# Layer 0 of a two-layer transformer kernel: the 4-bit weight codes unpacked in four groups of two pairs, and the second batch's preparation moved by a unit

## The chip, the cores and the metric

The kernel runs on one core of a Trainium2 chip, in one launch. The metric is the device time of a launch in microseconds. The engines are TensorE (PE), VectorE (DVE), ScalarE (ACT), GpSimd (POOL) and SyncE (SP), which issues the transfers.

## What is computed

Two layers, each an attention part and a feed-forward part on the same normalised input, over 8 batches of 256 tokens of width 256. The change touches layer 0 alone:

```python
xn = _layernorm(x)
# attention: 4 queries x 8 heads of width 8, K and V shared by the 4 queries
scores = einsum('bsqhd,bthd->bqhst', q, k) * scale
a_dot  = einsum('bqhst,bthd->bsqhd', softmax(scores), v)
a_mem  = elu(q) @ memory / (elu(q) @ memory_norm)
attn   = a_dot * (1 - w) + a_mem * w          # w = sigmoid(memory_weight)
# feed-forward: weights are 4-bit codes, two per byte, times a scale per 32
vals = LUT[stack([W & 15, W >> 4 & 15])] ; W = vals * scales
ffn  = (gelu(xn @ Wg.T) * (xn @ Wu.T)) @ Wd.T
x = x + attn + ffn
```

Layer 1 has another attention and a feed-forward with weights rounded to -1, 0 and 1 around a threshold taken from their mean absolute value. That mean is summed during layer 0.

## The kernel before

Layer 0 is a pipeline of **units**, one per batch and head: unit u works on batch u // 8 and head u % 8, and there are 64. Every engine runs its own program, a loop over u from `FIRST` = -3 to 66, and engines wait for one another by semaphores. In unit u TensorE does the exponentials' scores of unit u, the row scores of unit u + 2 (for the maximum), the gate and up products of chunk m = u - 1, the product with V of unit u - 1 and the down product of m - 2. ScalarE does the exponentials and the copies of high parts; VectorE the maxima (L593), the two GELU steps (L696, L704), the maxima's split into parts (L600, L602) and the normalisation (L612, L617); GpSimd multiplies hidden values (L345) and forms their low parts (L339). The split at L600 and L602, `split_max(u + 1)`, is the first thing that VectorE does in unit u, so in the text **unit u starts** at its L600, and unit u's length runs to the next L600. What TensorE does in a unit after its gate product waits for that split.

**Weights.** A pair a (0 to 7) is the 2 x 128 weight columns that chunk a uses. Its codes are 16-bit words, four codes each. `nibble_bits` (L620 on) moves the bits of the low and high codes into place as 8-bit floats; `decode(n)` (L638 on, n = 2a and 2a + 1) multiplies them by the loaded scales into an exact product of 768 columns; ScalarE copies its high part (L438) and GpSimd (L349, even n) and VectorE (L653, odd n) subtract to get the low part. Units -1 and 0 to 5 each decode one pair, and pair m is wanted by unit m + 1.

The bits are made in two halves of four pairs, each of five VectorE instructions over 1536 words: the first half at unit -3, two instructions of the second at the end of unit -1, the last two in unit 0. The codes lie in `probs`, a buffer of the exponentials, until they are spent; for that the exponential of unit 1 waits for `w_half` 5.

**A batch's preparation.** `schedule()` sets in which unit each step of a batch is done, on all engines: `stats` and `norm` (layer norm), `turn` (transposition on TensorE through the bank `misc`, high part by ScalarE, low part by VectorE at L543), `q`, `qlow`, `kv`, `mask0/1`, `recip0/1` (the division inside elu: L557, L559 on VectorE, L321, L324 on GpSimd), `mem` (two per batch, one for each 128 tokens: product with the memory into `misc`, L568 to L573 on VectorE) and `v` (V's transposition through `misc`). All steps in `FROM_MISC` use the same bank, so where a unit has two of them TensorE's second waits until the first has been read out (`evicted`):

```python
if before:
    evicted(*before)
...
elif kind == "mem":
    pe.wait_ge(S["mem_mul"], n + 1)
```

For batch 1 most steps stand a unit later than for the others (`late`), so that `mem` of batch 1 falls in units 8 and 9, and `v` in 9. From unit 9 to 17 VectorE also sums one piece of layer 1's weights (L684).

Of the kernel before, what the change touches and what calls it, by code (L numbers as in the profile page):

```python
# [15 lines left out]
P = 128  # L16
D = 256
# [57 lines left out]
SUM_AT, GAMMA_AT, SIGN_AT = 9, 21, 22  # L75
# [6 lines left out]
def schedule():  # L82

    at = {}

    def put(u, *step):
        at.setdefault(u, []).append(step)

    for kind in ("stats", "norm", "turn", "q", "qlow", "kv", "qload0", "mask0", "qload1", "mask1"):
        put(FIRST, kind, 0)  # L90
    put(-1, "recip0", 0)
    put(0, "recip1", 0)
    put(0, "v", 0)
    put(1, "mem", 0)
    put(2, "mem", 1)
    put(GAMMA_AT, "gamma", 0)
    for b in range(1, BATCH):
        late = int(b == 1)
        for n, kind in ((0, "stats"), (1, "norm"), (2 + late, "turn"), (3 + late, "q"), (4 + late, "qlow"), (4 + late, "qload0"), (4 + late, "kv"),
                        (5, "mask0"), (5 + late, "recip0"), (6 + late, "recip1"), (8, "qload1"), (8, "mask1")):  # L100
            put(HEADS * (b - 1) + n, kind, b)
        for t in range(2):
            put(HEADS * (b - 1) + 7 + late + t, "mem", 2 * b + t)
        put(HEADS * (b - 1) + 9, "v", b)
    for b in range(BATCH):
        put(HEADS * b + HEADS + 1, "att", b)
        put(HEADS * b + HEADS + LAG + BEHIND, "mlp", b)
    return at


def layer0(nc, dram, keep):
# [3 lines left out]
    with ExitStack() as ctx:  # L115
        def sb(name, shape, dt=F32):
# [43 lines left out]
        ones = sb("ones", [P, P])  # L160
# [6 lines left out]
        quarter = PAIRS_N * CW // 4  # L167
        codes, bits = ([spare[:, KC * 2 * D + quarter * n:KC * 2 * D + quarter * (n + 1)].bitcast(U16) for n in which] for which in ((0, 2), (1, 3)))
# [12 lines left out]
            codes0 codes1 stage0 stage1 w_half w2_hi_done w2_lo_even w2_lo_odd  # L181
# [20 lines left out]
        def _(sp):  # L202
# [10 lines left out]
            halves = dram["codes"].rearrange("p (h a) n -> p h (a n)", h=2)  # L213
            sp.dma_start(codes[0], halves[:, 0, :]).then_inc(S["codes0"], 16)
# [6 lines left out]
            sp.dma_start(codes[1], halves[:, 1, :]).then_inc(S["codes1"], 16)  # L221
# [80 lines left out]
        def _(pool):  # L302
# [6 lines left out]
            pool.memset(ones[:], 1.0).then_inc(S["zeroed"], 1)  # L309
# [55 lines left out]
            for u in range(FIRST, LAST):  # L365
                m = u - LAG
                if 0 <= m - 1 < M:
                    hidden_low(m - 1)
                if 0 <= m < M:
                    hidden(m)  # L370
                if 0 <= u + 2 < PAIRS_N and u >= 0:
                    weights_low(u + 2)
                for kind, n in at.get(u, []):
                    if kind == "mask1" and u == FIRST:
                        weights_low(0)
                    step(kind, n)
                    if kind == "recip0" and u == -1:
                        weights_low(1)
                i, odd = divmod(u - SIGN_AT - 1, 2)
                if 0 <= i < PIECES and not odd:  # L380
                    signs(i)

        @block.scalar
        def _(act):
# [3 lines left out]
            def step(kind, b):  # L388
# [10 lines left out]
                elif kind == "kv":  # L399
                    act.wait_ge(S["kv_done"], b + 1)  # L400
                    if b > 0:
                        for quad in range(2):
                            act.wait_ge(k_masked[quad], b)
                        act.wait_ge(S["v_turned"], b)
                    act.activation(kc[0:KROWS, :, :], misc[0:KROWS, :].rearrange("p (c n) -> p c n", c=2), ACT.Copy).then_inc(S["kv_copied"], 1)
                    act.activation(kc[KROWS:P, :, :].bitcast(F32), misc[KROWS:P, :].rearrange("p (c n) -> p c n", c=2), ACT.Copy).then_inc(S["kv_copied"], 1)
                elif kind == "v":
                    act.wait_ge(S["v_turned"], b + 1)
                    act.wait_ge(S["a_ready"], 4)
                    act.wait_ge(S["zeroed"], 5)  # L410
# [29 lines left out]
            def exponential(u, th):  # L440
                act.wait_ge(S["st_done"], 2 * u + th + 1)
                if u == 1 and th == 0:
                    act.wait_ge(S["w_half"], 5)
# [59 lines left out]
        def _(dve):  # L503
# [116 lines left out]
            def nibble_bits(half, n):  # L620

                at4 = slice(PAIRS_N // 2 * CW * half, PAIRS_N // 2 * CW * (half + 1))
                c, lo, hi, part = codes[half], low[:, at4], high[:, at4], bits[half]
                if n == 0:
                    dve.wait_ge(S[f"codes{half}"], 16)
                    dve.tensor_scalar(part, c, 2, 0x1C1C, ALU.logical_shift_left, ALU.bitwise_and).then_inc(S["dve_link"], 1)
                    dve.tensor_scalar(lo, c, 4, 0x8080, ALU.logical_shift_left, ALU.bitwise_and).then_inc(S["dve_link"], 1)
                    dve.wait_ge(S["dve_link"], linked(2))
                elif n == 1:
                    dve.tensor_tensor(lo, lo, part, ALU.bitwise_or).then_inc(S["dve_link"], 1)  # L630
                    dve.wait_ge(S["dve_link"], linked())
                elif n == 2:
                    dve.tensor_scalar(part, c, 2, 0x1C1C, ALU.logical_shift_right, ALU.bitwise_and).then_inc(S["dve_link"], 1)
                    dve.wait_ge(S["dve_link"], linked())
                else:
                    dve.scalar_tensor_tensor(out=hi, in0=c, scalar=0x8080, in1=part, op0=ALU.bitwise_and, op1=ALU.bitwise_or).then_inc(S["dve_link"], 1)
                    dve.wait_ge(S["dve_link"], linked())
# [24 lines left out]
            for u in range(FIRST, LAST):  # L662
                m = u - LAG
                if u == FIRST:
                    for kind, n in at[u]:
# [4 lines left out]
                        if kind == "turn":  # L670
                            for k in range(4):
                                nibble_bits(0, k)
# [52 lines left out]
        def _(pe):  # L725
# [33 lines left out]
            def step(kind, b):  # L759
# [1081 lines left out]
```

## Time and profile before

| | |
|---|---|
| time, median of 3 runs (lowest, highest) | 938.91 us (937.0, 942.07) |
| the profiled execution's own time | 938.2 us |
| its span | 936.4 us |
| PE busy | 763.0 us, 81% of the span |
| DVE busy | 699.5 us, 75% |
| ACT busy | 452.4 us, 48% |
| POOL busy | 419.0 us, 45% |
| instructions | 15623 |

The span is that of the engines in the profile; the run takes 1.8 us more around it. Layer 0 takes the first two thirds of the span. A row of the view in order of time gives start and duration, engine, line, operation, what is written and read, and in brackets how long the engine had been idle before, and what ended the wait.

### The profile page before, as it was taken

How to read it: one execution, taken by the hardware profiler on the slowest of the kernel's cores; microseconds unless marked ns; L12 is line 12 of the kernel's file. 1: busy time of each engine (PE TensorE's matmuls, PEld its weight loads, DVE VectorE, ACT ScalarE, POOL GpSimd, SP SyncE). 2: the span in 40 equal slices, each digit the busy share in tenths (PEclk: the TensorE clock that was granted, in tenths of full speed). 3: DMA queues.
4: the chain of work that ended last, by engine and by line, in shares of the span. 5: the costliest groups of instructions: out<-in, count | busy, mean ns of one | idle time of the engine just before them, and what ended most of it. 6: DMA issues, size and time to landing. Idle time of an engine off the chain costs nothing. (4 is left out here: it accounts for less than half of the span.)

```text
span 936.4 us, 15623 instructions
## 1 busy us (share of the span) xinstructions
PE 763.0 (81%) x5602; PEld 653.7 (70%) x5602; DVE 699.5 (75%) x1146; ACT 452.4 (48%) x717; POOL 419.0 (45%) x335
## 2 busy tenths in 40 slices
PE   3278989999999999999999999918683883893842
PEld 3166878888888888888888888806572672682642
DVE  6988866876776766776776766346689889879866
ACT  4256546556657556557556565535342342332301
POOL 2244533443466756662542543342616616606622
PEclk9999989999999999999999999958796896796775
DMA  4111210110110110110000000030000000000000
GB/s 150 34 35 36 86 42 25 53 42 2 30 36 19 47 42 19 47 30 3 20 18 12 11 19 3 1 147 1 1 1 0 8 15 0 0 22 0 0 22 23
DMA packets 21383, 25.82 MB, mean 28 GB/s; under 512 B 4418, under 2 KB 17090, under 8 KB 21060
## 3 DMA queue, kind: packets, MB, share of 16 engines
q1 hardware_dynamic: 21316, 24.93, 9.0%
q8 instruction: 41, 0.67, 0.3%
q14 instruction: 26, 0.21, 0.1%
HBM read 14.83 MB, written 3.28 MB: 19 GB/s over the span
## 5 line engine op out<-in xcount | busy, mean ns | idle before, releaser
L593 DVE TENSOR_REDUCE neg_max<-s_pair 128x4 f32<-128x1024 f32 x127 | 155.0, 1220 | 81.4 <-PE s_pair L805 81.1
L446 ACT ACTIVATE probs<-t_pair 128x1024 f32<-128x1024 f32 x128 | 131.3, 1026 | 139.8 <-PE t_pair L830 139.6
L345 POOL TENSOR_TENSOR hid<-g,hid 128x512 f32<-128x512 f32 x64 | 82.3, 1286 | 185.5 <-DVE g L704 143.9
L339 POOL TENSOR_TENSOR hid_lo<-hid,hid_hi 128x512 fp32r<-128x512 f32 x64 | 85.9, 1342 | 96.1 <-ACT hid_hi L456 96.0
L805 PE MATMUL s_pair<-K,Q 96*128 96x256 f32 x508 | 85.5, 292 | 14.0 <-DVE neg_max L593 9.4
L805 PEld LDWEIGHTS s_pair<-K,Q 96*128 96x128 f32 x508 | 76.6, 196 | 22.8 <-issue 7.3
L830 PE MATMUL t_pair<-Q,K 104*128 104x512 f32 x256 | 86.5, 420 | 0.3 <-DMA Q<-max_parts 0.3
L872 PE MATMUL down<-w_hi,hid_hi 128*128 128x256 f32 x256 | 83.9, 328 | 0.7 <-POOL hid_lo L339 0.7
L872 PE MATMUL down<-w_lo,hid_hi 128*128 128x256 f32 x256 | 72.1, 282 | 0.0
L872 PE MATMUL down<-w_hi,hid_lo 128*128 128x256 f32 x256 | 72.1, 282 | 0.0
L1151 POOL TENSOR_TENSOR rows<-rows,par 128x512 f32<-128x512 f32 x24 | 36.2, 1509 | 79.5 <-DVE rows L1499 52.4
L845 PE MATMUL misc<-probs,V 128*32 128x256 f32 x1024 | 69.1, 388 | 0.8 <-DVE xn_lo L543 0.5
L872 PEld LDWEIGHTS down<-w_hi,hid_hi 128*128 128x128 f32 x256 | 48.2, 188 | 26.4 <-issue 24.7
L1641 PE MATMUL lbank<-l_xn_hi,tern 128*128 128x512 f32 x96 | 38.0, 484 | 25.1 <-DVE l_hid L1469 25.1
L733 PE MATMUL gate<-xn_hi,w_hi 128*128 128x256 f32 x256 | 56.9, 304 | 0.0
L696 DVE SCALAR_TENSOR_TENSOR g<-g,gate 128x512 f32<-128x512 f32 x64 | 42.7, 668 | 18.6 <-ACT g L459 18.5
L467 ACT ACTIVATE g<-g 128x512 f32<-128x512 f32 x64 | 40.2, 628 | 26.6 <-DVE g L696 26.6
L733 PE MATMUL up<-xn_hi,w_hi 128*128 128x256 f32 x256 | 52.8, 289 | 0.0
L733 PE MATMUL up<-xn_lo,w_hi 128*128 128x256 f32 x256 | 52.3, 286 | 0.0
L733 PE MATMUL up<-xn_hi,w_lo 128*128 128x256 f32 x256 | 52.3, 287 | 0.0
L733 PE MATMUL gate<-xn_hi,w_lo 128*128 128x256 f32 x256 | 51.4, 282 | 0.0
L733 PE MATMUL gate<-xn_lo,w_hi 128*128 128x256 f32 x256 | 51.3, 282 | 0.0
(244 smaller groups left out, 2058.2 us busy)
## 6 DMA issues: line engine op xcount, KB each, us to landing
stage<-in_ternary SPq DMA_DIRECT2D x18, 256.0 KB, 2.9
Q<-q_hi SPq DMA_DIRECT2D x64, 64.0 KB, 2.0
stage<-in_scales SPq DMA_DIRECT2D x8, 384.0 KB, 3.4
X<-in_x SPq DMA_DIRECT2D x8, 256.0 KB, 3.7
Q<-q_lo SPq DMA_DIRECT2D x32, 64.0 KB, 2.0
Q<-max_parts SPq DMA_DIRECT2D x128, 4.0 KB
out<-res SPq DMA_DIRECT2D x8, 256.0 KB, 2.2
shared<-in_l1w SPq DMA_DIRECT2D x1, 1536.0 KB, 6.2
```

The lines of the kernel that those rows point to most:

```text
L339: pool.tensor_tensor(hid_lo[:, m % 2, :, :].rearrange("p a n -> p (a n)"), hid[:, m % 2, :], hid_hi[:, m % 2, :, :].rearrange("p a n -> p ...
L345: pool.tensor_tensor(hid[:, m % 2, :], g[:, m % 2, :], hid[:, m % 2, :], ALU.mult).then_inc(S["hid_done"], 1)
L446: act.activation(probs[:, u % 2, th, :], t_pair[:], ACT.Exp, scale=SCALE).then_inc(S["probs_done"], 1)
L467: act.activation(g[:, m % 2, :], g[:, m % 2, :], ACT.Tanh, scale=GELU_B).then_inc(S["t_done"], 1)
L593: dve.tensor_reduce(neg_max[:, u % 2, 4 * jp:4 * jp + 4], score_banks(u, jp)[:].rearrange("p (s n) -> p s n", n=SEQ), AX_X, ALU.max, negat ...
L696: dve.scalar_tensor_tensor(out=g[:, m % 2, :], in0=g[:, m % 2, :], scalar=1.0, in1=gate[:], op0=ALU.add, op1=ALU.mult).then_inc(S["u_done" ...
L733: mm = pe.matmul(out, lhs[a][k], rhs[b][k], start=(n == 0), stop=(n == 3 * KC - 1))
L805: mm = pe.matmul(score_banks(u, jp)[:, 512 * j + SEQ * s:512 * j + SEQ * s + SEQ], Q[0:KROWS, quad, 2 * jp + j, P * s:P * s + P], K[0:KROW ...
L830: mm = pe.matmul(t_pair[:, 512 * jp:512 * jp + 512].rearrange("p (j n) -> p j n", j=2), K[rows, quad, hq, P * th:P * th + P], Q[rows, quad ...
L845: mm = pe.matmul(misc[32 * j:32 * j + 32, 0:SEQ], V[:, th, h, :], probs[:, u % 2, th, SEQ * j:SEQ * j + SEQ], start=(th == 0), stop=(th == ...
L872: mm = pe.matmul(down[:, D * t:D * t + D], h[:, m % 2, n, P * t:P * t + P], w[:, a, n, 2 * D:3 * D], start=(a == 0 and t == 0 and n == 0 a ...
L1641: mm = pe.matmul(banks[bank][:], w[:, k, P * c:P * c + P], x[:, k, :], start=(n == 0), stop=(n == 3))
```

## The change

- The codes come by one transfer of 768 KB into `high` (in `X`, where the high bits are made in place) in place of two of 384 KB into `probs`. The transfer is fifth in SyncE's queue as the first half was.
- `nibble_bits(a)` handles two pairs: the same five instructions over 768 words, in `part`, a scratch of its own. It is called for pairs 0 and 1 in unit -3, for 2 and 3 at the end of unit -1, for 4 and 5 at the end of unit 1, for 6 and 7 at the end of unit 3, in the last two ahead of the unit's L653.
- In unit -1 `weights_low(1)` on VectorE follows the decodes at once. The memory's weights are scaled in unit 0.
- `schedule()`: batch 0's `recip0` in unit 0, `recip1` and `v` in 1, `mem` in 2 and 3 (before -1, 0, 0, 1 and 2). Batch 1's `stats` in unit 1 and `norm` in 2 (before 0 and 1); its `recip0`, `recip1` in 5 and 6 (before 6 and 7) and its `mem` in 7 and 8 (before 8 and 9). `turn`, `q`, `kv` and the masks stay.
- The sums of layer 1's weights begin in unit 10. `ones` lies in `part`, set when the weights are done. The exponential of unit 1 has no wait for `w_half`.

```diff
-SUM_AT, GAMMA_AT, SIGN_AT = 9, 21, 22
+SUM_AT, GAMMA_AT, SIGN_AT = 10, 21, 22
...
-    put(-1, "recip0", 0)
-    put(0, "recip1", 0)
-    put(0, "v", 0)
-    put(1, "mem", 0)
-    put(2, "mem", 1)
+    put(0, "recip0", 0)
+    put(1, "recip1", 0)
+    put(1, "v", 0)
+    put(2, "mem", 0)
+    put(3, "mem", 1)
...
-        for n, kind in ((0, "stats"), (1, "norm"), (2 + late, "turn"), (3 + late, "q"), (4 + late, "qlow"), (4 + late, "qload0"), (4 + late, "kv"),
-                        (5, "mask0"), (5 + late, "recip0"), (6 + late, "recip1"), (8, "qload1"), (8, "mask1")):
+        for n, kind in ((late, "stats"), (1 + late, "norm"), (2 + late, "turn"), (3 + late, "q"), (4 + late, "qlow"), (4 + late, "qload0"), (4 + late, "kv"),
+                        (5, "mask0"), (5, "recip0"), (6, "recip1"), (8, "qload1"), (8, "mask1")):
...
-            put(HEADS * (b - 1) + 7 + late + t, "mem", 2 * b + t)
+            put(HEADS * (b - 1) + 7 + t, "mem", 2 * b + t)
...
-            halves = dram["codes"].rearrange("p (h a) n -> p h (a n)", h=2)
-            sp.dma_start(codes[0], halves[:, 0, :]).then_inc(S["codes0"], 16)
+            sp.dma_start(high, dram["codes"].rearrange("p a n -> p (a n)")).then_inc(S["codes_loaded"], 16)
...
-            sp.dma_start(codes[1], halves[:, 1, :]).then_inc(S["codes1"], 16)
...
-                if u == 1 and th == 0:
-                    act.wait_ge(S["w_half"], 5)
...
+            def nibble_bits(a):
+
+                lo, hi = (x[:, CW * a:CW * a + 2 * CW] for x in (low, high))
+                dve.wait_ge(S["codes_loaded"], 16)
+                dve.tensor_scalar(part[:], hi, 2, 0x1C1C, ALU.logical_shift_left, ALU.bitwise_and).then_inc(S["dve_link"], 1)
+                dve.tensor_scalar(lo, hi, 4, 0x8080, ALU.logical_shift_left, ALU.bitwise_and).then_inc(S["dve_link"], 1)
+                dve.wait_ge(S["dve_link"], linked(2))
+                dve.tensor_tensor(lo, lo, part[:], ALU.bitwise_or).then_inc(S["dve_link"], 1)
+                dve.wait_ge(S["dve_link"], linked())
+                dve.tensor_scalar(part[:], hi, 2, 0x1C1C, ALU.logical_shift_right, ALU.bitwise_and).then_inc(S["dve_link"], 1)
+                dve.wait_ge(S["dve_link"], linked())
+                dve.scalar_tensor_tensor(out=hi, in0=hi, scalar=0x8080, in1=part[:], op0=ALU.bitwise_and, op1=ALU.bitwise_or).then_inc(S["dve_link"], 1)
+                dve.wait_ge(S["dve_link"], linked())
...
-                if u == 0:
-                    nibble_bits(1, 2)
-                    nibble_bits(1, 3)
...
                 if u == -1:
                     decode(2)
                     decode(3)
+                    weights_low(1)
+                    nibble_bits(2)
+                if u == 0:
                     memory_weights()
-                    for kind, n in at[u]:
-                        step(kind, n)
-                    weights_low(1)
-                    nibble_bits(1, 0)
-                    nibble_bits(1, 1)
+                if u in (1, 3):
+                    nibble_bits(u + 3)
                 if 0 <= u < PAIRS_N - 2:
                     weights_low(u + 2)
```

How the order moves, at three places. First VectorE from unit -1's decodes and the memory's weights to unit 0's, before (rows on probs and X of 1536 are the bits, xn<-q_neg is `recip`, stats and mv are `stats`):

```order
L557 TENSOR_SCALAR xn<-q_neg 128x256
L559 RECIPROCAL xn<-xn 128x256
L653 TENSOR_TENSOR w_lo<-hid,w_hi 128x768
L626 TENSOR_SCALAR probs<-probs 128x1536
L627 TENSOR_SCALAR X<-probs 128x1536
L630 TENSOR_TENSOR X<-X,probs 128x1536
L600 CAST max_parts<-misc 8x128
L602 TENSOR_TENSOR max_parts<-misc,max_parts 8x128
L557 TENSOR_SCALAR xn<-q_neg 128x256
L559 RECIPROCAL xn<-xn 128x256
L529 BN_STATS stats<-X 128x6 x2
L532 BN_AGGR mv<-stats 128x2 x2
```

After these come the last of the bits' instructions and the decodes.

VectorE now, from the same decodes of unit -1 (w_stage and hid are unit 0's `decode`):

```order
L645 TENSOR_TENSOR w_lo<-hid,w_hi 128x768
L621 TENSOR_SCALAR part<-X 128x768
L622 TENSOR_SCALAR X<-X 128x768
L624 TENSOR_TENSOR X<-X,part 128x768
L626 TENSOR_SCALAR part<-X 128x768
L628 SCALAR_TENSOR_TENSOR X<-X,part 128x768
L597 CAST max_parts<-misc 8x128
L599 TENSOR_TENSOR max_parts<-misc,max_parts 8x128
L554 TENSOR_SCALAR xn<-q_neg 128x256
L556 RECIPROCAL xn<-xn 128x256
L640 SCALAR_TENSOR_TENSOR w_stage<-X,stage 128x768
L640 SCALAR_TENSOR_TENSOR hid<-X,stage 128x768
```

The low part comes first, the bits are one group of 768, and one `recip` is left ahead of unit 0's decodes, where before `recip1`, `stats` and two of the bits' instructions stood.

Second, GpSimd from unit 0 to 2, before (q_neg and sigma are `recip`, rstd is `stats`, hid the hidden product, w_lo the low part of the weights):

```order
L321 TENSOR_TENSOR q_neg<-q_neg,xn 128x256
L324 TENSOR_TENSOR sigma<-sigma,q_neg 128x256
L315 TENSOR_SCALAR rstd<-mv 128x2
L317 TENSOR_TENSOR rstd<-rstd,half 128x2
L345 TENSOR_TENSOR hid<-g,hid 128x512
L349 TENSOR_TENSOR w_lo<-w_stage,w_hi 128x768
L339 TENSOR_TENSOR hid_lo<-hid,hid_hi 128x512
```

Both steps of `recip1` and the two of `stats` stand ahead of unit 1's hidden product. GpSimd now:

```order
L317 TENSOR_TENSOR q_neg<-q_neg,xn 128x256
L320 TENSOR_TENSOR sigma<-sigma,q_neg 128x256
L341 TENSOR_TENSOR hid<-g,hid 128x512
L345 TENSOR_TENSOR w_lo<-w_stage,w_hi 128x768
L317 TENSOR_TENSOR q_neg<-q_neg,xn 128x256
L320 TENSOR_TENSOR sigma<-sigma,q_neg 128x256
L311 TENSOR_SCALAR rstd<-mv 128x2
L313 TENSOR_TENSOR rstd<-rstd,half 128x2
L335 TENSOR_TENSOR hid_lo<-hid,hid_hi 128x512
```

`recip1` and `stats` have moved behind the hidden product and the low part of unit 1.

Third, TensorE in unit 3 now (mem is `mem`, ident with xn is `turn`):

```order
L721 MATMUL gate<-xn_lo,w_hi 128x256 x2
L775 MATMUL misc<-mem,sigma 128x130 x2
L752 MATMUL misc<-ident,xn 128x128 x4
L818 MATMUL t_pair<-Q,K 128x512 x2
L793 MATMUL s_pair<-K,Q 128x256 x4
```

Before, the row on mem stands in unit 2, and the row on xn follows the gate product. TensorE in unit 9 before (ident with kc is `v`):

```order
L733 MATMUL gate<-xn_lo,w_hi 128x256 x2
L787 MATMUL misc<-mem,sigma 128x130 x2
L781 MATMUL misc<-ident,kc 128x32 x4
L830 MATMUL t_pair<-Q,K 128x512 x2
L805 MATMUL s_pair<-K,Q 128x256 x4
```

Two steps use `misc` one after the other. Unit 9 now:

```order
L721 MATMUL gate<-xn_lo,w_hi 128x256 x2
L769 MATMUL misc<-ident,kc 128x32 x4
L818 MATMUL t_pair<-Q,K 128x512 x2
L793 MATMUL s_pair<-K,Q 128x256 x4
L721 MATMUL up<-xn_hi,w_hi 128x256 x2
```

A second step through `misc` stood in unit 9 and stands in unit 3 now.

## Rows read from the trace of the kernel before

**Rows 1.** Busy time by stretch; columns as the first line names them

```profile
core 0: us, PE busy (x) PEld busy (x) DVE busy (x) ACT busy (x) POOL busy (x), PEclk, DMA share, GB/s
60.00:70.00 10.00, 7.15 (x60) 5.74 (x59) 9.62 (x15) 6.20 (x10) 4.90 (x4) 1.00 0.14 40
...
134.00:136.00 2.00, 1.42 (x6) 1.26 (x7) 0.91 (x3) 0.37 (x1) 0.00 (x0) 0.50 0.00 0
```

**Rows 2.** VectorE's instructions in time, first half of the code bits (start, duration, us)

```profile
9.22 0.55 DVE L626 TENSOR_SCALAR probs<-probs 128x1536 uint16<-128x1536 uint16 x1
...
11.86 1.76 DVE L636 SCALAR_TENSOR_TENSOR X<-probs 128x1536 uint16<-128x1536 uint16 x1
13.71 0.69 DVE L547 TENSOR_TENSOR q_lo<-sigma,q_hi 128x512 fp32r<-128x512 f32 x1
```

**Rows 3.** VectorE's instructions in time, units -1 and 0

```profile
30.87 0.95 DVE L648 SCALAR_TENSOR_TENSOR hid<-X,stage 128x768 f32<-128x768 fp8e4 x1
...
32.38 0.29 DVE L557 TENSOR_SCALAR xn<-q_neg 128x256 f32<-128x256 f32 x1
...
34.37 0.90 DVE L653 TENSOR_TENSOR w_lo<-hid,w_hi 128x768 fp32r<-128x768 f32 x1
35.18 1.07 DVE L626 TENSOR_SCALAR probs<-probs 128x1536 uint16<-128x1536 uint16 x1
...
39.76 0.28 DVE L600 CAST max_parts<-misc 8x128 fp32r<-8x128 f32 x1
...
40.29 0.27 DVE L557 TENSOR_SCALAR xn<-q_neg 128x256 f32<-128x256 f32 x1
...
43.15 0.53 DVE L633 TENSOR_SCALAR probs<-probs 128x1536 uint16<-128x1536 uint16 x1
...
45.50 0.96 DVE L648 SCALAR_TENSOR_TENSOR w_stage<-X,stage 128x768 f32<-128x768 fp8e4 x1
...
52.19 0.28 DVE L600 CAST max_parts<-misc 8x128 fp32r<-8x128 f32 x1 [0.26 <-PE misc L817]
```

**Rows 4.** ScalarE's instructions in time, unit -1

```profile
31.85 0.84 ACT L438 ACTIVATE w_hi<-hid 128x768 fp32r<-128x768 f32 x1
```

**Rows 5.** VectorE's instructions in time, unit 1

```profile
52.71 0.72 DVE L539 TENSOR_SCALAR xn<-X,mv,rstd 128x256 f32<-128x256 f32 x2
...
56.08 0.42 DVE L570 TENSOR_TENSOR a_mem<-misc,a_rec 128x256 f32<-128x256 f32 x1
...
60.44 2.23 DVE L653 TENSOR_TENSOR w_lo<-X,w_hi 128x768 fp32r<-128x768 f32 x1
62.60 0.27 DVE L600 CAST max_parts<-misc 8x128 fp32r<-8x128 f32 x1
```

**Rows 6.** GpSimd's instructions in time, units 0 and 1

```profile
49.19 0.73 POOL L321 TENSOR_TENSOR q_neg<-q_neg,xn 128x256 f32<-128x256 f32 x1
...
51.09 1.40 POOL L317 TENSOR_TENSOR rstd<-rstd,half 128x2 f32<-128x2 f32 x1
...
60.03 1.83 POOL L349 TENSOR_TENSOR w_lo<-w_stage,w_hi 128x768 fp32r<-128x768 f32 x1
61.82 1.97 POOL L339 TENSOR_TENSOR hid_lo<-hid,hid_hi 128x512 fp32r<-128x512 f32 x1
```

**Rows 7.** TensorE's instructions in time, units 3 and 9

```profile
73.36 0.66 PE L764 MATMUL misc<-ident,xn 128*128 128x128 f32 x4 [1.61 <-DVE max_parts L602]
...
134.58 0.63 PE L781 MATMUL misc<-ident,kc 32*128 32x32 f32 x4 [3.58 <-DVE a_mem L570]
```

**Rows 8.** VectorE's instructions in time, units 4, 8 and 9

```profile
89.55 1.23 DVE L593 TENSOR_REDUCE neg_max<-s_pair 128x4 f32<-128x1024 f32 x1 [1.90 <-PE s_pair L805]
...
121.24 0.28 DVE L600 CAST max_parts<-misc 8x128 fp32r<-8x128 f32 x1 [0.63 <-PE misc L817]
...
129.64 0.28 DVE L600 CAST max_parts<-misc 8x128 fp32r<-8x128 f32 x1 [0.63 <-PE misc L817]
...
144.63 0.28 DVE L600 CAST max_parts<-misc 8x128 fp32r<-8x128 f32 x1 [0.62 <-PE misc L817]
```

More of the change, by code:

```diff
@@ L159, in layer0 @@
         below, sign = (w_stage[:].bitcast(BF16)[:, PIECE * n:PIECE * n + PIECE] for n in range(2))
-        ones = sb("ones", [P, P])
         hid_flat = hid[:].rearrange("p a n -> p (a n)")[:, 0:WORDS]
@@ L166, in layer0 @@
         w_raw = spare[:, 0:KC * 2 * D].rearrange("p (k n) -> p k n", k=KC)
-        quarter = PAIRS_N * CW // 4
-        codes, bits = ([spare[:, KC * 2 * D + quarter * n:KC * 2 * D + quarter * (n + 1)].bitcast(U16) for n in which] for which in ((0, 2), (1, 3)))
+        part = sb("part", [P, 2 * CW], U16)
+        ones = part[:, 0:2 * P].bitcast(F32)
         s_pair = ctx.enter_context(nc.psum_tensor("s_pair", [P, 1024], F32))
@@ L180, in layer0 @@
             gate_done up_done sq_done u_done t_done v1_done up_copied hid_done hid_hi_done hid_lo_done down_done
-            codes0 codes1 stage0 stage1 w_half w2_hi_done w2_lo_even w2_lo_odd
+            codes_loaded stage0 stage1 w_half w2_hi_done w2_lo_even w2_lo_odd
             summed gamma signed stored dve_link pool_link""".split()
@@ L308, in _ @@
             pool.memset(V[:, :, :, DH:DH + 1], 1.0).then_inc(S["zeroed"], 1)
-            pool.memset(ones[:], 1.0).then_inc(S["zeroed"], 1)
             def step(kind, b):
@@ L376, in _ @@
                     step(kind, n)
-                    if kind == "recip0" and u == -1:
-                        weights_low(1)
+                if u == -1:
+                    weights_low(1)
+                if u == SUM_AT:
+                    pool.wait_ge(S["w_half"], 2 * PAIRS_N)
+                    pool.memset(ones, 1.0).then_inc(S["zeroed"], 1)
                 i, odd = divmod(u - SIGN_AT - 1, 2)
@@ L409, in step @@
                     act.wait_ge(S["a_ready"], 4)
-                    act.wait_ge(S["zeroed"], 5)
+                    act.wait_ge(S["zeroed"], 4)
                     if b > 0:
@@ L618, in normalised @@
                                   ALU.mult).then_inc(S["o_normed"], 1)
[L620 to L637, printed above, removed]
+            def nibble_bits(a):
[10 more added lines that the diff above has]
+                dve.wait_ge(S["dve_link"], linked())
             def decode(n):
@@ L670, in _ @@
                         if kind == "turn":
-                            for k in range(4):
-                                nibble_bits(0, k)
+                            nibble_bits(0)
                     decode(0)
@@ L678, in _ @@
                 for kind, n in at.get(u, []):
-                    if kind not in FROM_MISC and u >= 0:
+                    if kind not in FROM_MISC:
                         step(kind, n)
@@ L713, in _ @@
                     decode(3)
+                    weights_low(1)
+                    nibble_bits(2)
+                if u == 0:
                     memory_weights()
-                    for kind, n in at[u]:
-                        step(kind, n)
-                    weights_low(1)
-                    nibble_bits(1, 0)
-                    nibble_bits(1, 1)
+                if u in (1, 3):
+                    nibble_bits(u + 3)
                 if 0 <= u < PAIRS_N - 2:
@@ L792, in step @@
                     pe.wait_ge(S["zeroed"], 5)
-                    pe.matmul(misc[:, 0:3], ones[:], gsum[:], start=True, stop=True).then_inc(S["gamma"], 1)
+                    pe.matmul(misc[:, 0:3], ones, gsum[:], start=True, stop=True).then_inc(S["gamma"], 1)
             def scores(u, jp):
```

## The prediction

> **What bounds the kernel now.** I read the view by stretch first: from 60 to 70 us VectorE is busy for 9.62 of 10 us and TensorE for 7.15 [rows 1]. So while the weights are being prepared (units -1 to 5) VectorE sets the pace, and an instruction added to it moves all that follows. The view in order of time then shows its rows without a bracket, that is with no wait ahead, for most of that stretch [rows 3, 5]; the exceptions are short (0.26 us at unit 1's start) or are TensorE's (1.90 us in unit 4) [rows 3, 8]. Behind these units the two engines hand one another their results, and a unit takes 8.40 us (unit 8, from 121.24 to 129.64). Unit 9 takes 14.99 us [rows 8]. TensorE's row tells why: it stood 3.58 us for `mem`'s multiplication on VectorE before it could use the bank again, and from 134 to 136 us its granted clock is 0.50, the 1.2 GHz level [rows 7, 1]. Layer 0 is one chain of units, so a unit's gain or loss arrives whole at the end. I add up, unit by unit, how far the start of each (its L600) moves against the profiled execution's own 938.2 us. The median of the runs is 0.7 us above that.
>
> **The price of a group.** One half now takes from 9.22 to 13.62 us, 4.40 us in five instructions [rows 2]. Its last takes 1.76 us for 1536 words, and a decode of 768 takes 0.95 [rows 2, 3], so the work halves and some 0.15 us per instruction stays: (4.40 - 0.75) / 2 + 0.75 = 2.6 us a group. The Trainium skill ("VectorE: DVE Perf Modes", section on the TRN2 errata) gives a fixed term of 58 cycles, 60 ns, per instruction; by it a group would be 2.35 us as an estimate and the sum 0.8 us less for the three groups that end up on the path. The trace shows more than that.
>
> **Unit -3.** The first group begins at 9.22 and ends at 11.8. The next instruction, q_lo, waits for ScalarE in any case and began at 13.71 [rows 2]. Gain: nothing. What covers it, 1.9 us, also covers a codes transfer that is twice as long, should it land late. The 768 KB load is ahead of the scales in SyncE's queue, but those are first used by the decodes, well behind q_lo.
>
> **Unit -1.** Decode ends at 31.82 [rows 3]. ScalarE's high part is done at 31.85 + 0.84 = 32.69 [rows 4], so `weights_low(1)` now waits 0.9 us where the memory's weights and `recip0` stood. It also meets GpSimd's low part, which takes 1.83 us and would run to 33.7. VectorE's subtraction took 0.90 us alone [rows 3] and 2.23 us where it met that one, ending 0.81 us after GpSimd's end at 61.86 [rows 5, 6]. So here it ends at 34.5, the second group at 37.1. Unit 0 starts 2.7 us **earlier** (before: 39.76 [rows 3]).
>
> **Unit 0.** Split 0.53 (39.76 to 40.29), one `recip` 1.99 (32.38 to 34.37), the memory's weights 0.56 (31.82 to 32.38), and what stood from 45.50 to 52.19 without its 0.26 wait, 6.43 [rows 3]: 9.5 us. Unit 1 starts at 46.6, 5.6 us **earlier**. That is where half the bits, `recip1` and `stats` have gone.
>
> **Unit 1.** Before, from 52.19 to 60.44, 8.25 us [rows 3, 5]. Out go `norm` (0.65) and `mem` (two of 0.42 and a small one, 1.0) [rows 5]; in come `recip1` and `stats`, 2.86 (40.29 to 43.15 [rows 3]): 9.5 us, to 56.1, a lead of 4.3 us. Now the third group and the low part follow, 3.5 us alone. But GpSimd has its queue at that moment: the hidden product and low part, which ended 1.42 us after this point before (61.86 against 60.44), so at 57.5 now; then `recip1` and `stats`, 3.3 us in the trace with some of it in collision (49.19 to 52.49), some 2.5 us free; then hid_lo, some 1.3 us free, 1.97 where it collides [rows 6]. All are operations that collide with VectorE's on SBUF. Taken strictly in turns from 57.5, 3.8 of GpSimd and 3.5 of VectorE end at 64.8; with no more collision than before it is 61.0. I take 63.7, near the first, because the order now puts five GpSimd instructions beside six of VectorE. Unit 2 starts 1.1 us **later** (-1.6 to +2.2; before 62.60 [rows 5]).
>
> **Unit 2.** `norm` comes in, GpSimd's collision at its start goes, TensorE starts at its low clock: +0.3 (0 to 1.2).
>
> **Unit 3, `mem` and `turn` together.** TensorE's second step must wait for VectorE's decodes, first GELU step and `mem`, about 4.1 us after the unit's start. It is unit 9's arrangement, which cost 14.99 - 8.40 = 6.6 us with the wait ending 4.9 us after the start [rows 7, 8]; 0.8 us less wait, and a little for the part of `turn` that was there, gives +5.5. Of this 3.0 is the wait itself, the rest the clock. A gap of 1.61 us ahead of the same `turn` did not halve the clock before: its four transposes took 0.66 us [rows 7]. Now the gap is nearly 3 us, with one short product ahead of it and 1.6 us of idle ahead of that. The fourth group adds 2.6 and some 0.2 of collision (up to 3.7). Unit 3: +8.3.
>
> **Unit 4.** It is TensorE's (1.90 us of VectorE waiting [rows 8]). The fourth group lets TensorE stand some 5 us before the unit starts, so its products begin at 1.2 GHz: +2.3 (0 to 3), a third of the 6.5 us from the split to the row at 89.55.
>
> **Units 5 to 9.** `recip0` of batch 1 comes into unit 5, 1.99 us, partly in a wait: +1.3 (0.6 to 2.0). Unit 6 exchanges one `recip` for the other: 0. Unit 7 gets a `mem`, 1.0, and loses a `recip` that was in a wait: +0.7 (0 to 1.0). Unit 8: the same length. Unit 9 keeps only `v` on the bank, as do later batches' units; I take it back to unit 8's length: **-6.6** (-6.0 to -6.9). Moving the sums by a unit, the scratch and the dropped exponential wait: 0, each beside other work.
>
> **Sum.** 1.1 + 0.3 + 5.5 + 2.8 + 2.3 + 1.3 + 0.7 - 6.6 = +7.4 us: 938.2 + 7.4 = **945.6 us**.
>
> **Rivals.**
> 1. *TensorE keeps its clock in units 3 and 4.* Then unit 3 loses 3.0 instead of 5.5 and unit 4 nothing: +2.6, **940.8 us**. For it: the 1.61 us gaps that left the clock up. Against it: the 3.58 us gap in unit 9 that did not. The decisive point is whether a broken gap of 3 us counts as one. The Trainium skill ("TensorE: Matmul & The Clock Gate", section on HAM oscillation) has the clock fall only when the idle stretch crosses a whole window of the gate, whose phase is free; by it this rival could be right in one run and wrong in another, at the same 940.8 us. Chance 0.22.
> 2. *Faster: the last two groups fall into time in which VectorE would have waited.* The lead of 4.3 us at the end of unit 1 is then kept: -4.3 + 0.3 + 3.0 + 1.3 + 0.7 - 6.6 = -5.6, **932.6 us**. It decides on whether VectorE has 2.6 us of waiting in units 1 and 3. Against it: 9.62 of 10 us busy, and no bracket at 60.44 or 62.60 [rows 1, 5]. For it: unit 3 will wait for TensorE anyhow, but ahead of the group and not where it stands. Chance 0.12.
> 3. *Slower still:* full turn-taking in units 1 and 3 and a low clock carried into unit 5: +2.2 + 1.2 + 5.8 + 3.7 + 3 + 2 + 1 - 6.0 = +12.9, **951 us**. Chance 0.06.
> 4. *It does not do what it says:* a code transfer later than its cover of 1.9 us, which would delay unit -2 by the rest. It is in the chance of the third.
>
> **How the numbers follow.** The forecast has 0.60. About 0.5% (4.7 us, 934.2 to 943.6) is what a measurement here can tell from no change. Faster: rival 2, 0.12. Same: rival 1 and the low edge of the forecast, 0.22 + 0.04 = 0.26. Slower: 0.56 + 0.06 = 0.62. The range takes in the forecast's bounds and most of rival 1: 939 to 950 us; left out are rival 2 and the far end, under 0.2.
>
> **What would show it.** Unit 0 should start near 37.1, unit 1 near 46.6, unit 2 near 63.7 with bits' instructions of twice their length beside GpSimd rows, unit 4 some 10 us later than before; TensorE's `turn` in unit 3 should wait for a_mem near 3 us with a granted clock of 0.50 behind it; unit 9 should be near 8.4 us. I am wrong if unit 1's end stays early, if unit 3 has no second wait, or if unit 9 stays at 15 us.

## The result and the profile after

| | before | changed |
|---|---|---|
| time, median (lowest, highest), 20 runs each | 937.08 us (933.3, 942.07) | 944.32 us (940.85, 949.73) |
| ratio of the mean times, 95% interval | | 1.0086 [1.0066, 1.0106] |
| the profiled execution's own time | 938.2 us | 949.73 us |

The changed kernel is slower by 0.9% (by 7.2 us, 0.8%, between the medians), and the whole interval lies above the 0.5% that a measurement here can tell. Its page begins:

```profile
span 947.8 us, 15633 instructions
...
PE 764.8 (81%) x5602; PEld 654.2 (69%) x5602; DVE 701.3 (74%) x1156; ACT 452.4 (48%) x717; POOL 416.6 (44%) x335
```

VectorE does 1.8 us more than before, TensorE 1.8 us: the work hardly grew. The profiled execution happens to be the longest of the 20, and its span is 11.4 us longer than before's. 3.1 us of that lie behind layer 0, where no instruction differs: from the start of unit 62 to the end of the span the trace has 352.0 us, before's 348.9, and those of the experiments below 345.6 to 351.0. So I compare layer 0, by the starts of its units (L597 here, L600 before). Unit 62 starts 8.3 us later than before, and all of that is there when unit 10 starts. Lengths in us, from one start to the next, and the sum of forecasts for the same units:

| unit | -1 | 0 | 1 | 2 | 3 | 4 | 5 | 6 | 7 | 8 | 9 |
|---|---|---|---|---|---|---|---|---|---|---|---|
| before | 13.93 | 12.43 | 10.41 | 10.12 | 9.71 | 11.24 | 11.16 | 8.72 | 7.69 | 8.40 | 14.99 |
| changed | 11.24 | 9.36 | 16.11 | 11.45 | 17.88 | 12.76 | 13.09 | 10.24 | 8.37 | 8.40 | 8.28 |
| difference | -2.7 | -3.1 | +5.7 | +1.3 | +8.2 | +1.5 | +1.9 | +1.5 | +0.7 | 0 | -6.7 |
| forecast | -2.7 | -2.9 | +6.7 | +0.3 | +8.3 | +2.3 | +1.3 | 0 | +0.7 | 0 | -6.6 |

The differences add up to +8.4 us, the forecasts to +7.4.

**Units -3 to 0.** VectorE's instructions in time (start, duration, what is written and read, in brackets the wait ahead):

```profile
9.21 0.35 DVE L621 TENSOR_SCALAR part<-X 128x768 uint16<-128x768 uint16 x1
...
10.85 0.96 DVE L628 SCALAR_TENSOR_TENSOR X<-X,part 128x768 uint16<-128x768 uint16 x1
13.70 0.69 DVE L544 TENSOR_TENSOR q_lo<-sigma,q_hi 128x512 fp32r<-128x512 f32 x1 [1.90 <-ACT q_hi L421]
...
32.72 1.80 DVE L645 TENSOR_TENSOR w_lo<-hid,w_hi 128x768 fp32r<-128x768 f32 x1 [0.91 <-ACT w_hi L437]
34.43 0.35 DVE L621 TENSOR_SCALAR part<-X 128x768 uint16<-128x768 uint16 x1
...
37.06 0.28 DVE L597 CAST max_parts<-misc 8x128 fp32r<-8x128 f32 x1
...
46.42 0.27 DVE L597 CAST max_parts<-misc 8x128 fp32r<-8x128 f32 x1
```

A group takes 2.63 us (34.43 to 37.06). In unit -3 q_lo starts where it did [rows 2] and the gain turns into 1.90 us of waiting, so the longer transfer was in time as well.

**Unit 1.** VectorE, then GpSimd, in time:

```profile
55.87 1.62 DVE L621 TENSOR_SCALAR part<-X 128x768 uint16<-128x768 uint16 x1
57.41 0.88 DVE L622 TENSOR_SCALAR X<-X 128x768 uint16<-128x768 uint16 x1
58.33 0.96 DVE L624 TENSOR_TENSOR X<-X,part 128x768 uint16<-128x768 uint16 x1
59.32 0.36 DVE L626 TENSOR_SCALAR part<-X 128x768 uint16<-128x768 uint16 x1
59.72 0.96 DVE L628 SCALAR_TENSOR_TENSOR X<-X,part 128x768 uint16<-128x768 uint16 x1
60.71 1.90 DVE L645 TENSOR_TENSOR w_lo<-X,w_hi 128x768 fp32r<-128x768 f32 x1
62.53 0.27 DVE L597 CAST max_parts<-misc 8x128 fp32r<-8x128 f32 x1
```

```profile
55.44 1.84 POOL L345 TENSOR_TENSOR w_lo<-w_stage,w_hi 128x768 fp32r<-128x768 f32 x1
57.22 0.85 POOL L317 TENSOR_TENSOR q_neg<-q_neg,xn 128x256 f32<-128x256 f32 x1
58.15 0.72 POOL L320 TENSOR_TENSOR sigma<-sigma,q_neg 128x256 f32<-128x256 f32 x1
58.96 0.38 POOL L311 TENSOR_SCALAR rstd<-mv 128x2 f32<-128x2 f32 x1
59.42 0.82 POOL L313 TENSOR_TENSOR rstd<-rstd,half 128x2 f32<-128x2 f32 x1
60.21 1.59 POOL L335 TENSOR_TENSOR hid_lo<-hid,hid_hi 128x512 fp32r<-128x512 f32 x1
```

The first instruction of the bits lasts 1.62 us in place of 0.35 and ends 0.2 us after GpSimd's low part (57.28). The Trainium skill ("SBUF — State Buffer", section "Who interferes with whom") says that where a VectorE instruction in one of its two-port modes meets one of GpSimd's, the one issued first keeps the shared ports to its end and the other waits; no row names the mode, but the length of this one agrees. The first three meet GpSimd and lose 2.2 us together, the low part 1.0; the fourth and fifth lose nothing, though `rstd`'s two small instructions stand beside them, and `hid_lo` begins beside the fifth. For the group and the low part VectorE took 6.7 us, where 3.5 would have done.

**Units 2 and 3.** TensorE in time, its stretches, and VectorE in time:

```profile
63.17 1.24 PE L775 MATMUL misc<-mem,sigma 128*128 128x130 f32 x4 [6.14 <-DVE max_parts L599]
...
74.62 0.71 PE L775 MATMUL misc<-mem,sigma 128*128 128x130 f32 x4 [1.10 <-DVE max_parts L599]
78.07 1.12 PE L752 MATMUL misc<-ident,xn 128*128 128x128 f32 x4 [2.74 <-DVE a_mem L567]
```

```profile
76.00:78.00 2.00, 0.00 (x0) 0.00 (x0) 1.97 (x4) 0.00 (x0) 0.00 (x0) 0.61 0.00 0
78.00:80.00 2.00, 1.93 (x7) 1.74 (x8) 0.59 (x3) 0.60 (x1) 0.00 (x0) 0.50 0.00 0
...
82.00:84.00 2.00, 2.00 (x19) 1.58 (x22) 0.76 (x2) 0.54 (x1) 0.00 (x0) 0.69 0.68 169
```

```profile
70.84 1.22 DVE L590 TENSOR_REDUCE neg_max<-s_pair 128x4 f32<-128x1024 f32 x1 [2.00 <-PE s_pair L793]
...
85.84 1.23 DVE L590 TENSOR_REDUCE neg_max<-s_pair 128x4 f32<-128x1024 f32 x1 [3.09 <-PE s_pair L793]
...
100.50 1.23 DVE L590 TENSOR_REDUCE neg_max<-s_pair 128x4 f32<-128x1024 f32 x1 [2.29 <-PE s_pair L793]
```

The new second wait is there: 2.74 us for `mem`'s multiplication on VectorE, after which the granted clock is 0.50 (1.2 GHz) and `turn`'s four transposes take 1.12 us where they took 0.66 [rows 7]. Unit 2 has a slow clock too (0.50 from 60 to 68 us): TensorE had stood 6.14 us while VectorE finished unit 1, its `mem` takes 1.24 us against 0.71 in unit 3, and VectorE waits 2.00 us for the scores at the unit's end.

**Unit 9.** VectorE's rows of two successive starts:

```profile
144.72 0.28 DVE L597 CAST max_parts<-misc 8x128 fp32r<-8x128 f32 x1 [0.63 <-PE misc L805]
...
153.00 0.28 DVE L597 CAST max_parts<-misc 8x128 fp32r<-8x128 f32 x1 [0.63 <-PE misc L805]
```

8.28 us, where it was 14.99 [rows 8]: the stall is gone from here.

### The profile page after: what moved, and what is told of

Same layout as the page of the kernel before. It is cut to its first block and busy times, and to the rows that moved or that the text cites. A ratio compares the mean times of both kernels' runs of the same rounds, so it can differ in the third digit from the quotient of the medians.

```text
span 947.8 us, 15633 instructions
## 1 busy us (share of the span) xinstructions
PE 764.8 (81%) x5602; PEld 654.2 (69%) x5602; DVE 701.3 (74%) x1156; ACT 452.4 (48%) x717; POOL 416.6 (44%) x335
## 3 DMA queue, kind: packets, MB, share of 16 engines
HBM read 14.83 MB, written 3.28 MB: 19 GB/s over the span
```

## The experiments

My theory: the time is set by *where* the steps stand. A step pair in one unit through `misc` costs some 6.6 us with its clock (gone in unit 9, new in unit 3), and bits that stand beside GpSimd's queue lose time in turns; the halved work of a group gains what it can only in the units before 1. The rival: TensorE's clock is the main price (rival 1 of the prediction with its sign turned), so that keeping it would take most of the loss away. A second rival: it is the mere number of instructions, fixed parts included, wherever they stand. In the tables "layer 0" is how far the start of unit 10 moves against before, counted from the start of unit -1; it is +8.4 us for the changed kernel. 1.5 us of this, in unit 6, come and go with the moment (last section); where a comparison needs it, they are taken out, which leaves +6.9.

### Batch 1's steps by themselves

Onto the kernel before (`b1early`), and taken back out of the changed one (`a_b1late`):

```diff
-                        (5, "mask0"), (5 + late, "recip0"), (6 + late, "recip1"), (8, "qload1"), (8, "mask1")):
+                        (5, "mask0"), (5, "recip0"), (6, "recip1"), (8, "qload1"), (8, "mask1")):
...
-            put(HEADS * (b - 1) + 7 + late + t, "mem", 2 * b + t)
+            put(HEADS * (b - 1) + 7 + t, "mem", 2 * b + t)
```

> The kernel before with one part of the change alone: batch 1's two reciprocals in units 5 and 6 and its mem in 7 and 8. Theory (a second step through the bank in unit 9 held TensorE for VectorE's mem): unit 9 falls from 15.0 to 8.9 us (it keeps its piece of the sum), unit 5 grows by 1.9, unit 7 by 0.7; in all 3.5 us faster, ratio 0.996. Rival (unit 9 is long for the sum and the layer norm there): unit 9 stays over 13 us and the kernel is 1 to 3 us slower, ratio 1.002.

> The changed kernel with that same part undone: batch 1's reciprocals in 6 and 7, mem in 8 and 9. Theory: unit 9 goes back to some 14.4 us (no sum in it), units 5 and 7 lose 1.9 and 0.7: some 3.5 us slower than the changed kernel, layer 0 some 12 us longer than before, ratio to before 1.012. Rival (the gain in unit 9 came from the sum that moved to unit 10): unit 9 stays under 9 us and the kernel is 2.6 us faster than the changed one, ratio 1.006.

| | median | ratio to before | units 5, 6, 7, 9 | layer 0 |
|---|---|---|---|---|
| b1early | 935.17 us | 0.9958 [0.9936, 0.9981] | 13.08, 10.18, 8.38, 8.54 | -2.4 us |
| a_b1late | 948.44 us | 1.0094 [1.0067, 1.0121] | 11.15, 8.72, 7.68, 14.83 | +10.4 us |

This part alone makes the kernel faster, and without it layer 0 is longer still in the trace (+10.4 us). The ratios of `a_b1late` and of the changed kernel, 1.0094 and 1.0086, don't tell these two apart; 1.012 had been expected. Unit 9 gives 6.5 us in both; unit 5 takes 1.9, unit 7 0.7 and unit 6 1.5 of it back. In `a_b1late` TensorE has the second wait of unit 9 again:

```profile
144.54 0.63 PE L769 MATMUL misc<-ident,kc 32*128 32x32 f32 x4 [2.98 <-DVE a_mem L567]
```

### Batch 0's preparation back where it was

```diff
-    put(0, "recip0", 0)
-    put(1, "recip1", 0)
-    put(1, "v", 0)
-    put(2, "mem", 0)
-    put(3, "mem", 1)
+    put(-1, "recip0", 0)
+    put(0, "recip1", 0)
+    put(0, "v", 0)
+    put(1, "mem", 0)
+    put(2, "mem", 1)
...
-                    if kind not in FROM_MISC:
+                    if kind not in FROM_MISC and u >= 0:
                         step(kind, n)
...
                     weights_low(1)
+                    memory_weights()
+                    for kind, n in at[u]:
+                        step(kind, n)
                     nibble_bits(2)
-                if u == 0:
-                    memory_weights()
```

> The changed kernel with batch 0's steps where they were before (reciprocals in units -1 and 0, v in 0, mem in 1 and 2), the bits still in four groups. Theory (mem and turn of unit 3 on one bank, and GpSimd's steps beside the bits in unit 1): unit 3 falls from 17.9 to about 12.5, unit 1 from 16.1 by 2.9 for the reciprocal and by some 1 for the collision while 1.0 comes back with mem; units -1 and 0 grow by 2.6 and 0. Layer 0 is 1 to 2.5 us longer than before, ratio 1.002. Rival (the groups of bits alone are what costs): unit 3 stays over 16 us and layer 0 is 7 to 8 us longer than before, ratio 1.008.

942.02 us, ratio 1.004 [1.0011, 1.0069], layer 0 +5.3 us. Unit 3 takes 13.30 us in place of 17.88: 4.6 us for the second step through `misc`, in the same unit and with the same group of bits. Units 1 and 2 are shorter too, by 1.8 and 1.0, and unit -1 is longer by 4.2. In all, the later preparation of batch 0 costs 3.1 us. The expectation had 1 to 2.5 us for layer 0 and missed it: unit 3 stays 0.8 us above the expected 12.5, and unit -1 grows by 4.2 in place of 2.6.

### The bits alone

`a_b0early` with batch 1's schedule of before, `stats` and `norm` included, so that the groups of two pairs are nearly all that is left of the change:

```diff
-        for n, kind in ((late, "stats"), (1 + late, "norm"), (2 + late, "turn"), (3 + late, "q"), (4 + late, "qlow"), (4 + late, "qload0"), (4 + late, "kv"),
-                        (5, "mask0"), (5, "recip0"), (6, "recip1"), (8, "qload1"), (8, "mask1")):
+        for n, kind in ((0, "stats"), (1, "norm"), (2 + late, "turn"), (3 + late, "q"), (4 + late, "qlow"), (4 + late, "qload0"), (4 + late, "kv"),
+                        (5, "mask0"), (5 + late, "recip0"), (6 + late, "recip1"), (8, "qload1"), (8, "mask1")):
...
-            put(HEADS * (b - 1) + 7 + t, "mem", 2 * b + t)
+            put(HEADS * (b - 1) + 7 + late + t, "mem", 2 * b + t)
```

> The bits in four groups over the schedule of the kernel before, with every batch step where it was. Theory (the four groups cost more than the two halves because the third and fourth stand on VectorE at the ends of units 1 and 3, and TensorE's clock falls in the gaps they make): units -1 and 0 together 1.8 us shorter, unit 1 3.9 longer, unit 3 3.6, unit 4 1.9, unit 9 15 us as before; layer 0 some 8 us longer, ratio 1.008. Rival (the groups cost little by themselves, the loss is all in the schedule): ratio within 1.002.

945.95 us, ratio 1.0075 [1.005, 1.01], layer 0 +9.7 us. Against before: unit -1 +1.5, unit 0 -2.4, unit 1 +3.7, unit 2 +1.1, unit 3 +3.6, unit 4 +2.3. The two halves cost VectorE 2 x 4.4 us at free lengths and four groups 4 x 2.63 = 10.5, 1.7 us more. But the first half stood in unit -3, where it cost nothing (q_lo starts at 13.7 us with the half and with the group), and of the four groups only one does. On the path there were 4.4 us and are 3 x 2.63 = 7.9, so 3.5 of the 9.7 us are instructions. The other 6 are waits and collisions, and hang on where the groups stand; the next runs test that.

### The same bits in another place

`a_bits0` moves the third and fourth group to the end of unit 0. `a_bits0pool1` has GpSimd, besides, do unit 1's steps ahead of its hidden product, and `a_pool1` does that alone.

```diff
-                if u in (1, 3):
-                    nibble_bits(u + 3)
+                if u == 0:
+                    nibble_bits(4)
+                    nibble_bits(6)
```

```diff
+                if u == 1:
+                    for kind, n in at[u]:
+                        step(kind, n)
                 if 0 <= m - 1 < M:
                     hidden_low(m - 1)
                 if 0 <= m < M:
                     hidden(m)
...
-                    step(kind, n)
+                    if u != 1:
+                        step(kind, n)
```

> The changed kernel with the third and fourth groups at the end of unit 0, where GpSimd is idle and no chunk has begun. Theory (place, not work): unit 0 grows by two groups, 5.0 us; unit 1 falls by 2.6 and some 1.0 of collision, unit 3 by 3.6 with what collided, unit 4 by 1 to 2 for TensorE's clock: 3 to 4 us faster than the changed kernel, ratio 1.005. Rival (only the sum of instructions counts): no change against the changed kernel, ratio 1.0086.

> The changed kernel with GpSimd doing recip1 and stats of unit 1 ahead of that unit's hidden product, when it is idle. No work changes. Theory (VectorE's bits in unit 1 wait for GpSimd's instructions one by one): the bits' first three instructions lose their long durations but one, unit 1 falls from 16.1 to about 14.8, ratio to before 1.007. Rival (the bits are slow for another reason, such as the new scratch): unit 1 stays 16.1.

> Both edits at once: the third and fourth groups at the end of unit 0, and GpSimd's recip1 and stats of unit 1 ahead of its hidden product. Theory (in the kernel with the groups in unit 0, unit 2 took 13.2 us because norm waited 1.97 us for GpSimd's stats behind its hidden product and low part, and mem's product for recip1): unit 2 falls from 13.2 to about 10.8, layer 0 by 2 to 2.5 us against that kernel, ratio to before 1.002. Rival (unit 2 was long for TensorE's clock alone): unit 2 stays over 12.5 us and the ratio is 1.0045.

| | median | ratio to before | units 0, 1, 2, 3, 4 | layer 0 |
|---|---|---|---|---|
| a_bits0 | 941.29 us | 1.0046 [1.0019, 1.0073] | 14.64, 11.59, 13.21, 14.15, 11.24 | +4.6 us |
| a_pool1 | 945.33 us | 1.0061 [1.0035, 1.0086] | 9.35, 15.64, 11.16, 17.76, 12.75 | +7.5 us |
| a_bits0pool1 | 937.41 us | 0.9996 [0.9977, 1.0015] | 14.65, 11.93, 10.65, 13.86, 11.23 | +2.1 us |

No instruction of the changed kernel is taken away in any of the three, and the last is 0.9% faster than it, level with the kernel before, where 1.002 had been expected: the second rival (number of instructions) falls. In `a_bits0` all ten instructions of the two groups have their free lengths. Unit 1 is 4.5 us shorter, unit 3 3.7, unit 4 1.5; unit 0 is 5.3 longer, unit 2 is 1.8 longer, and units 5 and 6 together are 0.5 longer than with unit 6's clock kept. So the place is worth 2 us, and 4.8 with the next edit. Unit 2 grows since its `norm` now waits for what GpSimd has last in its queue:

```profile
65.98 1.68 DVE L536 TENSOR_SCALAR xn<-X,mv,rstd 128x256 f32<-128x256 f32 x2 [1.97 <-POOL rstd L313]
```

With GpSimd's steps moved ahead, in `a_bits0pool1`, that row has no wait:

```profile
64.12 1.16 DVE L540 TENSOR_SCALAR xn<-X,mv,rstd 128x256 f32<-128x256 f32 x2
```

`a_pool1` missed its expectation for unit 1: 15.64 us, where 14.8 had been expected. VectorE's first two of the bits there:

```profile
56.58 1.61 DVE L625 TENSOR_SCALAR part<-X 128x768 uint16<-128x768 uint16 x1
58.11 1.42 DVE L626 TENSOR_SCALAR X<-X 128x768 uint16<-128x768 uint16 x1
```

The number of GpSimd instructions beside them fell from six to two, but GpSimd's two long ones (the low parts of the weights, 1.83 us, and of the hidden values, 1.38 us) each hold one of VectorE's short ones, 2.3 us together. After them everything is at free length. With six beside them VectorE lost 3.2 us, with two 2.3. So most of the cost goes with the long instructions that one meets, and little with how many there are.

### TensorE kept busy in unit 3

22 products with a discarded result stand between `mem` and `turn`, in the 2.7 us of waiting:

```diff
                     if before:
+                        if u == 3:
+                            pe.wait_ge(S["up_copied"], u - LAG)
+                            for _ in range(22):
+                                pe.matmul(up[:, 0:SEQ], w_hi[:, 0, 0, 0:P], xn_hi[:, 0, 0, :], start=True, stop=True)
                         evicted(*before)
```

> The changed kernel with 22 products added on TensorE in unit 3, into the bank up, in the time in which it waits for VectorE's mem. Their result is overwritten unread. Theory (of the 8 us by which unit 3 grew some 2.5 are TensorE's clock): the granted clock stays 1.00 from 74 to 84 us and unit 3 falls from 17.9 to about 15.4, ratio to before 1.006. Rival (the clock lies beside VectorE's work and costs nothing): unit 3 keeps 17.9 us or grows by the products that run past the wait, ratio 1.009 or more.

946.21 us, ratio 1.0078 [1.0049, 1.0107], which can't be told from the changed kernel's 1.0086. TensorE in time, and its stretch, with this edit:

```profile
73.55 2.88 PE L876 MATMUL up<-xn_hi,w_hi 128*128 128x256 f32 x22
76.54 0.66 PE L752 MATMUL misc<-ident,xn 128*128 128x128 f32 x4
```

```profile
78.00:80.00 2.00, 2.00 (x26) 1.70 (x28) 2.00 (x3) 1.64 (x3) 0.00 (x0) 1.00 0.02 4
```

The clock stays up, and unit 3 is 15.57 us in place of 17.88. So of the 4.6 us of that unit's second step 2.3 are the clock; the rest I put down to the wait. But unit 4 takes 13.99 us in place of 12.76: half of the gain is lost again there. TensorE stands 3.75 us ahead of it in both kernels, and with the edit the granted clock is down at once (0.51 from 88 to 90 us; 0.87 from 92 to 94 us in the changed kernel); why it fell sooner no run shows. The profiled execution is also the fastest of its six (939.9 us), so its units can't be read as those of the median. The rival falls: with the clock kept in unit 3 (and, by chance, in unit 6) layer 0 is still 5.3 us longer than before.

### A version that beats both

`best1` takes what has been shown to be good: the kernel before with `b1early`'s edit, and the bits of unit -1 ahead of `recip0` and the low part, where GpSimd has nothing to do yet:

```diff
                     memory_weights()
+                    nibble_bits(1, 0)
+                    nibble_bits(1, 1)
                     for kind, n in at[u]:
                         step(kind, n)
                     weights_low(1)
-                    nibble_bits(1, 0)
-                    nibble_bits(1, 1)
```

> The kernel before with batch 1's reciprocals and mem a unit earlier, and in unit -1 the two instructions' worth of bits ahead of recip0 and the low part, so that GpSimd is idle beside them. Theory: the bits' three instructions fall from 4.6 to 2.1 us, the low part gains some of it back by meeting GpSimd's; unit -1 some 1.5 to 2 us shorter on top of the 3.9 of the schedule: ratio to before 0.994. Rival (the collision only moves to the low part and to unit 0): ratio 0.996 as with the schedule alone.

932.33 us (930.76 to 933.62), ratio 0.992 [0.9888, 0.9952]: faster than both kernels. Layer 0 is 6.3 us shorter when unit 10 starts. VectorE in time, unit -1:

```profile
32.41 0.55 DVE L626 TENSOR_SCALAR probs<-probs 128x1536 uint16<-128x1536 uint16 x1
...
33.47 0.96 DVE L630 TENSOR_TENSOR X<-X,probs 128x1536 uint16<-128x1536 uint16 x1
...
36.46 0.89 DVE L653 TENSOR_TENSOR w_lo<-hid,w_hi 128x768 fp32r<-128x768 f32 x1
```

The first of these took 1.07 us before [rows 3]. Unit -1 is 11.41 us in place of 13.93, from this order alone and nearly as short as with half the bits gone (11.24).

## Why the prediction was right, and where its terms were off

The forecast, 945.6 us and slower, held: 944.32 us were measured. That the medians moved by 7.2 us, so near to the forecast's +7.4, is in part luck: terms that were too dear by 1.8 us and too cheap by 3.1 offset one another, and layer 0 in the trace moved by 8.4. By its steps:

- **Unit -3, the price of a group, unit -1, unit 0**: right to 0.2 us (2.63 us a group; starts at 37.06 and 46.42 against 37.1 and 46.6). The lower price by the Trainium skill ("VectorE: DVE Perf Modes", TRN2 errata), 2.35 us a group, isn't what this trace has; the same section notes that the measured fixed term is nearer 150 cycles than its 58. The same instruction at 1536 and 768 words took 0.55 and 0.35 us, which leaves 0.15 for the part that doesn't halve.
- **Unit 1**: a term mis-sized. I let nearly all of GpSimd's 3.8 us and VectorE's 3.5 us run in turns, and put the start of unit 2 at 63.7. It was 62.53, 0.1 us *earlier* than before. Of the two ends that I had set, 61.0 and 64.8, the truth lay between, since two of five instructions of the bits escaped; `a_pool1` and `a_bits0` show that the long GpSimd instructions do the holding.
- **Unit 2, +0.3**: mis-sized, +1.3. I had named TensorE's low clock here and given it no more than 1.2 us. Its gap of 6.14 us shows in VectorE's wait of 2.00 us; that wait is 0.24 us in `a_bits0pool1`, whose granted clock stays at 1.00 in this unit.
- **Unit 3, `mem` and `turn` together, +5.5, and the fourth group, +2.8**: their sum was right, +8.2. The wait forecast as 3.0 us was 2.74, with the clock at 0.50 behind it. The experiments divide it otherwise: 4.6 us for the two steps and 3.6 for the group with its collision (`a_bitsonly`, unit 3). So my analogy with unit 9 gave the two steps 0.9 too much, and the group 0.8 too little.
- **Unit 4, +2.3**: +1.5. TensorE stood 3.75 us, not 5. That this is the fourth group's doing is shown by `a_bits0`, in which unit 4 is back at 11.24.
- **Unit 5, +1.3**: +1.9, and the same in all but two of the kernels that have `recip0` there (in `a_bits0` and `a_bits0pool1` unit 5 is +3.8 and unit 6 -1.4). Of the 1.99 us some 0.8 did go into a wait for TensorE (1.40 us before, 0.57 now), but the low part at the unit's end now meets GpSimd for longer (1.90 us, 1.07 before) and takes it back.
- **Unit 6, 0**: wrong by 1.5 us, the largest miss. The granted clock fell to 0.50 there behind a gap of 1.90 us; the last section has what is known of it.
- **Units 7 and 9**: right (+0.7; -6.7 against -6.6).

The sum was 1 us short, with units 1 and 4 too dear by 1.8 and units 2, 5 and 6 too cheap by 3.1. The rivals: *TensorE keeps its clock* is refuted for what the kernel does by the granted clock, and for what it would be worth by `a_warm3`: 2.3 us in unit 3 less 1.2 in unit 4, against the 2.5 and 2.3 that I had given it. *The last groups fall into waiting time* is refuted by `a_bits0`: without the groups its units 1 and 3 are 4.5 and 3.7 us shorter, so they stood in no waiting time there. *Slower still* had its terms for units 1, 3 and 4 too high (+2.2, +5.8 and +3 against -0.1, +4.6 and +1.5). The late transfer isn't seen.

By parts, with unit 6 held at the length before: four groups of bits in place of two halves +9.7 us, batch 1's steps a unit earlier -3.8 (-3.5 taken out of the changed kernel), batch 0's a unit later +3.1. What is left of the sum to +6.9, some -2, is `stats` and `norm` of batch 1. No run changed them alone, but in units 0 to 4 `a_bitsonly` differs from `a_b0early` in nothing else, and is 1.8 us longer there.

## What to carry to other kernels

A shared bank that two steps use in one unit costs the second wait and the clock behind it, here 4.6 us in unit 3 and 6.5 in unit 9; look for every unit where a moved step meets another one in the same bank, before counting what it leaves behind. Instructions that are short by themselves are best put where the other engine on SBUF has nothing long in its queue: the same two groups were 2 us cheaper in unit 0, 2.5 more with GpSimd's order mended, and in unit -1 a change of order alone was worth 2.5 us. A change of several parts should be timed by parts: here one part that gains 4 us was buried under two that lose more.

## What the runs showed that I had not expected

The same idle time doesn't always bring the clock down. `b1early` and `best1` have the same unit 6, 2.6 us apart in time. TensorE's row there, and its stretches, in `b1early`:

```profile
108.81 0.91 PE L805 MATMUL s_pair<-K,Q 96*128 96x256 f32 x4 [1.89 <-issue]
```

```profile
108.00:110.00 2.00, 1.19 (x7) 1.22 (x8) 1.97 (x2) 0.00 (x1) 1.92 (x3) 0.78 0.02 4
110.00:112.00 2.00, 2.00 (x11) 1.99 (x10) 2.00 (x3) 0.63 (x1) 1.50 (x2) 0.50 0.96 268
```

and in `best1`:

```profile
106.20 0.72 PE L805 MATMUL s_pair<-K,Q 96*128 96x256 f32 x4 [1.88 <-issue]
```

```profile
106.00:108.00 2.00, 1.80 (x15) 1.83 (x16) 1.97 (x3) 0.00 (x0) 1.92 (x4) 1.00 0.27 48
108.00:110.00 2.00, 2.00 (x25) 1.28 (x25) 2.00 (x4) 1.38 (x3) 0.90 (x1) 1.00 1.00 310
```

A gap of 1.9 us in both, ahead of the same work; behind it the clock falls to 0.50 in one and stays at 1.00 in the other, and the unit takes 10.18 us or 8.73. The Trainium skill ("TensorE: Matmul & The Clock Gate", section "What's actually happening") says that the window in which TensorE's activity is judged runs freely, whenever the kernel starts, so that the moment has a part in it; these rows fit that and don't prove it. Of the eight kernels with a gap of 1.9 us in unit 6 four fell to 0.50 (changed, `b1early`, `a_b0early`, `a_pool1`) and four stayed (`a_b1late`, `a_bitsonly`, `a_warm3`, `best1`); before, the gap was 1.07 us and the clock stayed. Units 31 and 39 show the same: 11.67 and 10.18 us before, 10.15 and 10.16 in `b1early`, 11.66 and 11.69 in `best1`; in unit 31 TensorE's gap is 1.51 us before and in `b1early`, and behind it the clock is 0.50 in the one (328 to 330 us) and 1.00 in the other. Each such unit moves a kernel by 1.5 us, also where no edit touched it. So a difference of 1 to 2 us here is read from the unit that was edited, or from many runs, and not from one trace's end.
